# Sum over the states of batches 0 to 2 kept turned, with an accumulating transpose of each product

## The reference, cut to what matters

```
step(h, (u_t, d_t, B_t, C_t)):
    dA = exp(d_t[..., None] * A)                              # 128 channels x 16 states
    h  = dA * h + (d_t * u_t)[..., None] * B_t[:, None, :]
    y  = einsum('bdn,bn->bd', h, C_t)                         # sum over the 16 states
y = ys + u * D
y = y * silu(z)                                               # z: the gate, a projection of LN(x)
return y @ out_proj_w.T
```

## Time and profile before

| | |
|---|---|
| median of 3 runs | 388.09 us (387.36 to 388.6) |
| span of the profiled execution | 397.8 us |
| busy: DVE, PE, POOL, ACT | 310.1, 316.1, 282.1, 233.3 us |
| mean granted TensorE clock | 0.868 |
| PE on the sum over the states, line 984 | 124.9 us busy, 256 records |

### The profile page before, as it was taken

One profiled execution on the slowest core, in us unless ns is written; L12 is line 12 of the kernel. 1 busy time (PEld: TensorE's weight loads), 2 busy tenths in 40 slices (PEclk: granted clock), 3 DMA queues, 4 the chain that ended last, 5 costly groups with the idle time before them and its releaser, 6 DMA issues. The chain is left out here.

```text
span 397.8 us, 4347 instructions
## 1 busy us (share of the span) xinstructions
PE 316.1 (79%) x1257; PEld 188.4 (47%) x1257; DVE 310.1 (78%) x360; ACT 233.3 (59%) x519; POOL 282.1 (71%) x201
## 2 busy tenths in 40 slices
PE   7832986957989896897989698796895798869784
PEld 3311432313535352553545265363773576748764
DVE  4799987999999999987999989999981157425441
ACT  4456797524798984659797268775651455234221
POOL 3435846987993999999599999966877044745760
PEclk9965897999998998879899898989987599968955
DMA  4287999999798699856878769997210900000000
GB/s 99 36 281 248 274 243 366 390 200 368 315 315 323 208 308 297 284 190 244 303 254 298 203 175 325 318 369 226 61 30 19 250 23 4 18 8 17 16 1 8
DMA packets 43986, 78.68 MB, mean 198 GB/s; under 512 B 16050, under 2 KB 26093, under 8 KB 43962
## 3 DMA queue, kind: packets, MB, share of 16 engines
q1 hardware_dynamic: 41066, 73.88, 57.5%
q0 software_dynamic: 2896, 4.53, 4.2%
HBM read 72.30 MB, written 7.54 MB: 201 GB/s over the span
## 5 line engine op out<-in xcount | busy, mean ns | idle before, releaser
L518 POOL TENSOR_TENSOR prod<-h,csb 128x1024 f32<-128x1024 f32 (+1 forms) x64 | 143.7, 2253 | 24.9 <-DMA csb<-bc_rows 10.5
L984 PE MATMUL Yp<-prod,ident 128*128 128x512 f32 (+1 forms) x256 | 124.9, 624 | 13.8 <-POOL prod L518 13.6
L1318 DVE TENSOR_TENSOR_SCAN h<-dA,Bp 128x1024 f32<-128x1024 f32 (+2 forms) x58 | 119.7, 2064 | 4.7 <-DVE Bp L1277 1.0
L984 PEld LDWEIGHTS Yp<-prod,ident 128*128 128x128 f32 x256 | 50.3, 208 | 75.3 <-issue 50.3
L697 ACT ACTIVATE dA<-delta,aneg 128x1024 f32<-128x1024 f32 (+1 forms) x58 | 62.9, 1093 | 23.1 <-DVE h L1318 19.0
L1277 DVE TENSOR_TENSOR Bp<-Cp,bsb 128x1024 f32<-128x1024 f32 (+1 forms) x58 | 67.7, 1168 | 6.4 <-DMA bsb<-bc_rows 4.2
L615 POOL DMA_INDIRECT out_dram<-dA,csb x30 | 30.3, 1009 | 36.5 <-DVE dA L1509 28.9
L558 POOL DMA_INDIRECT slots<-rows_,slot x30 | 30.1, 1002 | 6.9 <-issue 4.5
L1495 DVE TENSOR_TENSOR dA<-Bp,b2s 128x320 f32<-128x320 f32 (+1 forms) x8 | 3.8, 475 | 33.8 <-PE Bp L1167 15.6
L1153 PE MATMUL Cp<-prod,w1s 128*128 128x384 f32 (+1 forms) x64 | 24.7, 508 | 2.0 <-issue 2.0
L895 ACT ACTIVATE bsb<-Yp,b1c 128x256 f32<-128x256 f32 x16 | 7.6, 475 | 23.4 <-PE Yp L1184 14.0
(11 more groups left out here) (290 smaller groups left out, 604.8 us busy)
## 6 DMA issues: line engine op xcount, KB each, us to landing
bsb<-bc_rows SPq DMA_DIRECT2D x48, 512.0 KB, 6.7
csb<-bc_rows SPq DMA_DIRECT2D x48, 512.0 KB
bsb<-bc_rows SPq DMA_DIRECT2D x16, 384.0 KB, 5.7
csb<-bc_rows SPq DMA_DIRECT2D x16, 384.0 KB
slots<-fill POOLq DMA_DIRECT2D x1, 2600.0 KB
csb<-slots SPq DMA_DIRECT2D x6, 325.0 KB, 5.3
bcs<-bc_rows SPq DMA_DIRECT2D x2, 512.0 KB, 10.9
xs_in<-in_x_dram SPq DMA_DIRECT2D x1, 768.0 KB, 5.8
```

What stands on the lines that cost most here:

```text
L518: po.tensor_tensor(prod[:, k % 4, c], h[:, k % 3, c], csb[:, k % CSLOTS, c], ALU.mult).then_inc(s_pP, 1)
L984: ins = te_.matmul(Yp[:, c], idn, prod[:, k % 4, c], start=False, stop=(n == 15), skip_group_check=True)
L1318: ins = ve.tensor_tensor_scan(h[:, k % 3, c], decays, drives, h[:, k % 3, c.start - 1:c.start] if i else 0.0, ALU.mult, ALU.add)
```

## The change

For units v < CARRY the sum is kept turned: tokens on the partitions, 128 channels along the row, one tile of 128 x 128 for each 128 tokens.

- Each state's product is added by 8 transposes with accumulation (product tile stationary, identity moving) in place of 2 matmuls of 512 columns.
- The sum is opened by 8 matmuls with a tile of u stationary and diag(D) moving.
- The gate of batches 0 to 2 is made turned: a tile of the normed input is stationary, the gate weights are moving, 4 matmuls of 128 columns for each one of 512.
- DVE's product of sum and gate has the same shape and is now turned. PE turns it back with 8 transposes into Yp (b_yr), ACT copies the two halves from PSUM into yt (b_yT), and the output projection reads yt as before. PE's wait for b_yg now stands ahead of the skip matmuls.

```diff
@@ ACT, back
+                if n == 1 and v < CARRY:
+                    for q in range(2):
+                        act.wait_ge(b_yr, 2 * v + q + 1)
+                        ac.activation(yt[:, HB[q]], Yp[:, HB[q]], ACT.Copy).then_inc(b_yT, 1)
@@ PE, front (n 10, 11)
-                    te_.matmul(bank(f, "gate", q), wzT[:, :], xnT[0:C, f % 3, 3 + q * HALF:3 + (q + 1) * HALF], start=True,
-                               stop=True).then_inc(f_mz, 1)
+                    x = 3 + q * HALF
+                    if f == B - 1:
+                        ins = te_.matmul(bank(f, "gate", q), wzT[:, :], xnT[0:C, f % 3, x:x + HALF], start=True, stop=True)
+                    else:
+                        for t in range(4):
+                            ins = te_.matmul(bank(f, "gate", q)[:, t * P:(t + 1) * P], xnT[0:C, f % 3, x + t * P:x + (t + 1) * P],
+                                             wzT[:, :], start=True, stop=True)
+                    ins.then_inc(f_mz, 1)
@@ PE, open_sum
+                if v >= CARRY:
+                    te_.matmul(Yp[:, c], diagD[:, :], u[:, UNITS[v][0] % 2, c], start=True, stop=False, skip_group_check=True)
+                    return
+                for x in range(c.start, c.stop, P):
+                    te_.matmul(Yp[:, x:x + P], u[:, UNITS[v][0] % 2, x:x + P], diagD[:, :], start=(x == c.start), stop=False,
+                               skip_group_check=True)
@@ PE, add_state
+                if v < CARRY:
+                    for x in range(0, L, P):
+                        ins = te_.matmul(Yp[:, x:x + P], prod[:, k % 4, x:x + P], idn, is_transpose=True, start=False,
+                                         stop=(n == 15), skip_group_check=True)
+                else:
+                    for c in pieces(v):
+                        ins = te_.matmul(Yp[:, c], idn, prod[:, k % 4, c], start=False, stop=(n == 15),
+                                         skip_group_check=True)
@@ PE, back (n 1)
+                    if v < CARRY:
+                        pe.wait_ge(b_yg, v + 1)
+                        for q in range(2):
+                            for t in range(4):
+                                x = (4 * q + t) * P
+                                ins = te_.transpose(Yp[:, x:x + P], yt[:, x:x + P], idn)
+                            ins.then_inc(b_yr, 1)
                     for t in range(nt):
                         tok = 3 + (t0 + t) * P
                         te_.matmul(mixer_bank(v)[:, t * C:(t + 1) * C], xnT[0:C, b % 3, tok:tok + P], sk[:, :], start=(t == 0),
                                    stop=False, skip_group_check=True)
                     pe.wait_ge(b_yg, v + 1)
                     if v < CARRY:
+                        pe.wait_ge(b_yT, 2 * v + 2)
                         pe.wait_ge(f_silu, UNITS[v + 1][0] + 1)
...
```

More of the change, by code:

```diff
@@ L235, in metaformer_layer @@
         p_bx, p_dA, p_half = map(sem, "p_bx p_dA p_half".split())
+        b_yr, b_yT = sem("b_yr"), sem("b_yT")
         (b_yg, b_op, b_sq, b_y2, b_rs, b_n2, b_tr, b_n2T, b_pr, b_t1, b_tr3, b_h3T, b_lg, b_cg, b_rs3,
@@ L969, in front @@
                         pe.wait_ge(f_zr, 2 * f - 1)
-                    te_.matmul(bank(f, "gate", q), wzT[:, :], xnT[0:C, f % 3, 3 + q * HALF:3 + (q + 1) * HALF], start=True,
-                               stop=True).then_inc(f_mz, 1)
-            def open_sum(v, c):
-                te_.matmul(Yp[:, c], diagD[:, :], u[:, UNITS[v][0] % 2, c], start=True, stop=False, skip_group_check=True)
+                    x = 3 + q * HALF
[6 more added lines that the diff above has]
+                    ins.then_inc(f_mz, 1)
+            def open_sum(v, c):
+                if v >= CARRY:
[4 more added lines that the diff above has]
+                               skip_group_check=True)
             def add_state(v, n):
@@ L982, in add_state @@
                 pe.wait_ge(s_pP, k + 1)
-                for c in pieces(v):
-                    ins = te_.matmul(Yp[:, c], idn, prod[:, k % 4, c], start=False, stop=(n == 15),
-                                     skip_group_check=True)
+                if v < CARRY:
[6 more added lines that the diff above has]
+                                         skip_group_check=True)
                 ins.then_inc(s_sum, 1)
@@ L1100, in _ @@
             for q in range(2):
-                te_.matmul(Cp[:, HB[q]], wzT[:, :], xnT[0:C, 0, 3 + q * HALF:3 + (q + 1) * HALF], start=True,
-                           stop=True).then_inc(f_mz, 1)
+                for t in range(4 * q, 4 * q + 4):
+                    ins = te_.matmul(Cp[:, t * P:(t + 1) * P], xnT[0:C, 0, 3 + t * P:3 + (t + 1) * P], wzT[:, :], start=True,
+                                     stop=True)
+                ins.then_inc(f_mz, 1)
             pe.wait_ge(w_in, 16 * 9)
```

## The result

| | before | after |
|---|---|---|
| median, us | 388.3 (387.36 to 388.6) | 406.86 (403.43 to 412.38) |
| ratio, 95% interval | | 1.046 [1.041, 1.052] |
| span of the profiled execution, us | 397.8 | 401.7 |
| mean granted TensorE clock | 0.868 | 0.779 |
| busy, us: DVE, PE | 310.1, 316.1 | 310.7, 302.1 |

The change costs 18.6 us in the median. The forecast was 402.2, range 391.5 to 408: the direction, the likeliest case and that range held. The forecast came out 4.7 us short, and the narrower range that it gave the likeliest case, 399 to 406, was missed by 0.9.

What follows compares the result with a forecast made beforehand. DVE bounds the states, and the way back makes it late at three boundaries: 16.7 us at half clock, taken as 14.5 for a late clock fall, times 0.976 = 14.1, so 402.2 us; range 391.5 to 408, own range 399 to 406.

Steps and rivals of the forecast that it cites:

- the likeliest case: TensorE at half clock at all three unit boundaries: 402.2 us, own range 399 to 406, chance 0.60.
- What bounds the kernel, and the chain: States bound by DVE; a chain yt, projection, squares, pooled decay, scan of state 5 can make DVE late at each boundary.
- The sum: Each state's sum on PE: eight transposes, 0.9 us at full clock, 1.89 at half, against 1.88; worth at most 3.9 us.
- Rival 4: Accumulating fp32 transposes go as two records, a state's sum stays at 1.8 us, clock unchanged: 396.4 us, chance 0.06.
- Which clock: Clock 0.50 ahead of the first boundary and likeliest half at all three; a late fall saves up to 1.1 us each.
- The boundaries: DVE's added standing at the three unit boundaries: 6.6 + 3.3 + 6.8 = 16.7 us lost at half clock.
- The full-clock terms: Net loss at the three boundaries at full clock: 2.8 - 0.6 + 2.4 = 4.6 us.
- Rival 1: Full clock at the boundaries: 4.6 x 0.976 = 4.5 us lost, 392.6 us, chance 0.18.
- Rivals 2 and 5: 2: chain not longer, DVE's 3.37 and 0.51 us vanish, 384.3 us, chance 0.04. 5: unseen slack, within 0.3%, chance 0.06.
- Rival 3: PE becomes the bound at half clock, 72.7 us in a batch of 60: 413 us, chance 0.06.
- ACT's other waits: ACT waiting elsewhere for a slower PE: up to 2 us in the range, which its lead of two decays should hide.
- the conversion from profile to median, 0.976: Median 388.09 over profiled 397.8 us, a ratio of 0.976; scales the 14.5 us loss to 14.1.

Runs made afterwards that it cites:

- the run that held the clock up: Changed kernel plus zero matmuls in states 11 to 15 and behind the turning-back transposes, skip matmuls ahead of the b_yg wait: 395.89 us, ratio 1.027 against before.

## Why the prediction was right, and where it was short

**What bounds the kernel, and the chain: right.** DVE's busy time is 310.7 us against 310.1. What it lost in the states of the profiled execution is standing: 18.0 + 1.4 us, against 3.37 + 0.51, 15.5 more. The last of the 16 scans of the last unit starts (source views of their lines, first and last start) at 313.6 where it was 298.4, 15.2 later:

```profile
L1297 DVE TENSOR_TENSOR_SCAN h<-dA,hl,Bp x16: 722/730/747, 277.9 to 298.4; 128x256 f32<-128x256 f32 x16
```
```profile
L1328 DVE TENSOR_TENSOR_SCAN h<-dA,hl,Bp x16: 720/730/747, 293.7 to 313.6; 128x256 f32<-128x256 f32 x16
```

**The sum: right.** One record a transpose, 1.04 us a state at full clock (0.9 predicted), 1.97 at half (1.89). Rival 4, two records, falls by the count of 384. Its gain was put at nothing but the 3.9 us that DVE stood before, and the removed wait at yt is all of it that came: 0.51.

**Which clock: right in outcome, not quite in course.** Half clock ruled the projections of all three boundaries (means of 0.56, 0.66 and 0.55 from yt to the projection's end), and the last states of batch 0 were at 0.50 as foreseen; but the clock came back at 98 us and fell again at 101.7, at yt. At the second and third boundary the fall was late, as the prediction allowed: the turn back still ran in 1.06 and 1.07 us. Why the clock falls at a boundary is not settled. The prediction laid it, for the first one, on the shorter sums. These do lower the clock ahead of that boundary, but with two records a tile or doubled transposes, at 0.94 and 0.91 over 45 to 100 us, it fell there all the same, to 0.52 and 0.54 during the projection. Of the runs with the way back only those with the added matmuls of zeros kept a projection at 1.00.

**The boundaries: right at the first and third.** Net of what before lost, half clock was to cost 6.6 + 3.3 + 6.8; measured 6.14, 4.67 - 3.37 = 1.30, and 7.16 - 0.51 = 6.65. The second was put 2 us too high: its projection was to end 12.0 us behind yt and ended 10.07 behind it, since the clock fell late and was back at 1.00 from 180.4, before the projection's end. In all that is 14.1 against 14.5 taken. That the sum came out so well is in part luck: of the 2.6 us below the 16.7 of a full half clock 2.0 came from this one boundary, to which the prediction allowed 1.1. The full-clock terms were borne out by the run that held the clock up: 2.64 + 2.64 + 3.05 less the 3.9 of before is 4.4, against 4.6. So 9.7 of the 14.1 us go with the low clock. The skip path, which that run also moves, isn't what did it: where it was left in its place, the two boundaries that stayed at 1.00 cost 2.64 and 3.06. Rival 1 is therefore priced right in what DVE stands, but isn't what happens unaided. Rivals 2 and 5 fall with the first boundary. Rival 3 falls with the doubled transposes.

**Mis-sized, 1.4 us: ACT's other waits.** The prediction kept them at nothing in the sum, up to 2 us in the range, since ACT leads by two decays. The lead did not quite hide them: 1.4 us at line 698, two waits.

**Wrong, but worth only 0.3 us: the conversion from profile to median, 0.976.** It assumed that the profiled execution of before was slow all through, so that a loss in it shrinks in the median. But a time is 1.7 to 1.9 us above its span in each of the executions where both are listed (403.43 and 401.7 in after), so that one took about 399.5 us, 11.4 above the median, and 11.3 of these lay in one place, the experts. From the end of the last scan (298.4 + 0.7) to the end of the span it took 98.7 us, and after took 401.7 - 314.3 = 87.4; no other profiled execution here took more. The tail of before has a wait, put down to no engine of the core, that the tail of after hasn't and that may be most of it:

```profile
DVE dA L1495 <- remote: 14.9, 2, 10.8
```

So a loss among the states counts in full. 388.1 + 15.5 = 403.6, and the profiled execution of after took 403.43. That the scaled forecast, 14.1, equals the net standing at the boundaries is chance: 14.5 was 0.4 high, and the factor took off about as much.

**Not settled: the median.** The other executions of after took 405.5 to 412.4, and 404.4 to 411.0 in the longer series. In both the profiled one was the fastest, so what the slower ones lose, 3 us in the median and the larger part of the 4.7 that the forecast was short, stands in no trace. Their mean clocks (0.766 to 0.785) hardly differ from its 0.779. That they stand longer at the second boundary, as the prediction had it (6.7 us in place of 4.67), would give 2 of it, but that is only argued.

**POOL was held up, at no cost seen.** The prediction said that this would make it wrong. A wait of POOL for PE's line 1001 ended at 116.09; DVE was standing for ACT from 114.28 to 120.42 anyway.

```profile
116.09 2.35 POOL L519 TENSOR_TENSOR prod<-h,csb 128x1024 f32<-128x1024 f32 x1 [2.30 <-PE Yp L1001]
```

## What to carry to other kernels

Before a step is added to a chain that crosses engines, price it at the boundary where it stands, with the queue that each engine has ahead of it: PE's sum went from 124.9 to 69.7 us and gained half a microsecond, while eight transposes and two copies at three boundaries cost 15. Read the clock on that chain too: at 1.00 the boundaries made DVE stand 8.3 us in place of 18.0. A lighter TensorE need not make a faster kernel: more work on it (matmul sums, doubled transposes) made this one faster in the median, though the traces show only part of why. And take a difference between a profiled execution and the median apart by stage before scaling by it; it may lie where the change isn't.

## What the runs showed of the hardware

Accumulating fp32 transposes raise TensorE's clock: 0.69 to 0.91 over 45 to 100 us when their number was doubled and nothing else added. The same program meets the fall of the clock at different places from one execution to the next: in one profiled execution of after the turn back of the first boundary ran at half clock, in 1.94 us, and in the other at full, in 1.07. Code that a change left alone can meet it differently too: the second boundary ran at 0.61 in before and at 1.00 with batch 0 alone turned, for 8.74 and 3.95 us from yt to the projection's end. The executions of before ranged from 383.7 to 395.0 us in one series; how much of that comes from it, no run tells.
